# Side work in pairs behind two units' scores, and another order at the ending, in a fused differential attention and feed-forward kernel

## The chip, the cores and the metric

The kernel runs on one core of a Trainium2 chip. The metric is the time of one execution on the device in microseconds. Engine names: TensorE (PE) multiplies, VectorE (DVE) and GpSimd (POOL) do elementwise work, ScalarE (ACT) evaluates functions such as the exponential, and SP only issues transfers (DMAs). Every engine works through its own list in order and waits on semaphores.

## The reference

One sequence of 1024 rows of 256 numbers is normalised and goes through two branches, whose results are added to the input:

```python
xn = layernorm(x)
qkv = xn @ Wqkv                       # q1, k1, q2, k2: 16 heads of 8; v: 16 heads of 16
A1 = causal_softmax(q1 k1) v
A2 = causal_softmax(q2 k2) v
diff = A1 - lam * A2                  # lam from four small vectors
diff = (1 - LAMBDA_INIT) * diff / rms(diff)
attn = diff @ Wproj
ffn  = (gelu(fp8(xn) @ fp8(Wg0)) * (fp8(xn) @ fp8(Wg1))) @ fp8(Wlinear)
out  = x + attn + ffn
```

## The kernel before

**Start.** The rows are normalised and transposed; queries and keys of the first branch are projected and split into an upper and a lower part (`upper` on ScalarE copies the upper part, `rest` on VectorE subtracts it, L621 to 626). `x_to_fp8` (L628) casts the normalised rows in two halves for the feed-forward. The feed-forward's first product runs as 16 steps (L951 to 972), each four products on TensorE, a Gelu on ScalarE (L473) and a gated product on VectorE (L644). Step n waits for the gated product of the last step in the same PSUM banks: the first three steps have banks of their own, and the fourth waits for the first's gated product.

**Attention.** The scores of 2 branches x 4 groups of heads are cut into 96 *units* (12 for each of 8 groups). A unit is three banks of 512 scores. For each unit TensorE computes scores (`scores`, L1027, three or six products, one for each stretch of keys, in row tiles of 32 x 128), ScalarE takes one exponential of 128 x 1536 (L497), and GpSimd zeroes what lies above the diagonal. Units use two sets of three PSUM banks in turn, so the scores of unit n wait for the exponential of unit n - 2 (`exp_done`, L1040).

**Side work.** After the scores of unit n TensorE does that unit's *side work* in column tiles of 128 x 32: `values_due` (L1106) multiplies exponentials of an earlier unit with the values into bank 6, from where VectorE takes them (`take`, L719), and `beside` (L974) does projections that the tables `V_AT`, `QK_AT`, `NORM_AT` and `DOWN_AT` assign to the unit: values, queries and keys of the second branch, norms, and the feed-forward's second product. The tables are written by hand so that nearly every unit has one chunk of values or something of that size. Each float32 product is two passes on TensorE. The loop is in `attention` (L1114).

**Ending.** After the last exponential, TensorE (`ending`, L1141) finishes the values and projects them: `project(b, p)` for 8 blocks b of rows and two halves p of the heads. The products with p = 0 need nothing new; those with p = 1 wait for VectorE to have turned the last group's result back (`turn_back`, L766, which counts `out_t_ready`). ScalarE copies blocks 0, 1 and 6 out of PSUM (`whole`, L501) and between them takes the square root on which the last 16 blocks of rows wait (L513). VectorE adds the residual to the other blocks (L879, L882), and SP and ScalarE send the result out.

## Time and profile before

| | |
|---|---|
| median of 3 runs | 184.3 us (184.03 to 184.45) |
| the profiled execution | 184.12 us, its span 182.3 us |
| TensorE busy | 175.5 us, 96% |
| ScalarE busy | 163.2 us, 90% |
| VectorE busy | 92.4 us, 51% |
| GpSimd busy | 63.5 us, 35% |
| exponentials (L497) | 97 of them, 138.1 us together |
| granted TensorE clock | 0.999 of 2.4 GHz |

The span is from the first to the last instruction. Busy shares are averages over three stages: the start up to the first exponential at 32.9 us, the attention up to the end of the last exponential at 171.2 us, and the ending. The end of a matmul is modelled in the trace, so TensorE looks denser than it is; starts are to be trusted more.

### The profile page before, as it was taken

What the parts mean: (1) busy time and instruction counts of PE and PEld (TensorE: products, weight loads), DVE (VectorE), ACT (ScalarE), POOL (GpSimd) and SP (SyncE); (2) the same over time, 40 slices, a digit from 0 to 9 for tenths busy, and PEclk for the clock granted to TensorE, in tenths of its full rate; (3) what the DMA queues carried; (4) which work ended last, traced back from release to release, by engine and by line L of the source; (5) the groups of instructions that cost most, each with busy time, mean ns of one, the idle gap of its engine ahead of it and who ended that gap; (6) DMA issues with size and microseconds to landing.
All of it is one profiled execution on the core that took longest, in us unless ns stands there. A gap on an engine that the chain in (4) does not pass through costs nothing.

```text
span 182.3 us, 4305 instructions
## 1 busy us (share of the span) xinstructions
PE 175.5 (96%) x1816; PEld 76.3 (42%) x1816; DVE 92.4 (51%) x219; ACT 163.2 (90%) x146; POOL 63.5 (35%) x81
## 2 busy tenths in 40 slices
PE   6999999999999999999999999999999999989992
PEld 6785344543332333343234434334524434432481
DVE  1878789312233230640374121706542789979982
ACT  3586678999999999999999999999999999999820
POOL 8449920052017322360622063217303560323000
PEclk9999999999999999999999999999999999999999
DMA  5996888780000000000277875000000000000015
GB/s 152 382 333 227 219 197 201 175 189 19 0 0 5 0 0 4 0 4 0 42 204 179 210 173 127 0 0 4 4 0 0 4 0 4 0 0 4 0 58 180
DMA packets 8935, 15.02 MB, mean 82 GB/s; under 512 B 2000, under 2 KB 5584, under 8 KB 8912
## 3 DMA queue, kind: packets, MB, share of 16 engines
q1 hardware_dynamic: 8080, 13.92, 28.0%
q10 hardware_dynamic: 832, 0.79, 1.3%
q8 instruction: 16, 0.26, 0.6%
q14 instruction: 7, 0.06, 0.1%
HBM read 5.26 MB, written 1.05 MB: 35 GB/s over the span
## 4 chain that ended last, share of the span: by engine, by line
PE 82%; DVE 11%; ACT 2%; DMA 2%; issue 1%; DVEq 0%
PE ps L1062 35%; PE ps L1050 20%; PE ps L904 12%; PE ps L970 7%; PE ps L1098 4%; DVE o_t L719 2%; PE ps L914 2%; DMA x_sb<-L_attn_x 2%; DVE parts L625 1%; PE ps L894 1%; PE ps L1103 1%; DVE parts L737 1%; ACT L455 1%; DVE area L630 1%; DVE xn_t L763 1%
## 5 line engine op out<-in xcount | busy, mean ns | idle before, releaser
L497 ACT ACTIVATE probs<-ps,shift 128x1536 f32<-128x1536 f32 (+1 forms) x97 | 138.1, 1582 | 0.2 <-PE ps L1050 0.2
L1062 PE MATMUL ps<-probs,v_all 128*32 128x512 f32 (+3 forms) x776 | 78.1, 492 | 1.0 <-DVE o_t L719 0.8
L393 POOL TENSOR_SCALAR_AFFINE_SELECT probs<-probs 128x1024 f32<-128x1024 f32 (+1 forms) x40 | 36.7, 918 | 94.9 <-ACT probs L497 94.8
L1050 PE MATMUL ps<-q_st,k_st 32*128 32x512 f32 (+3 forms) x384 | 48.3, 411 | 0.0
L1050 PEld LDWEIGHTS ps<-q_st,k_st 32*128 32x128 f32 x384 | 22.5, 182 | 61.5 <-ACT probs L497 43.4
L719 DVE STREAM_TRANSPOSE o_t<-ps 128x512 f32<-128x512 f32 x16 | 11.5, 717 | 45.0 <-PE ps L1062 45.0
L1062 PEld LDWEIGHTS ps<-probs,v_all 128*32 128x32 f32 x776 | 16.4, 108 | 18.7 <-issue 9.7
L970 PE MATMUL ps<-area 128*128 128x512 fp8e4 x64 | 14.4, 379 | 0.2 <-DVE parts L625 0.2
L473 ACT ACTIVATE probs<-ps 128x512 bf16<-128x512 f32 x16 | 9.6, 597 | 3.7 <-PE ps L970 3.1
L644 DVE TENSOR_TENSOR area<-ps,probs 128x512 fp8e4<-128x512 f32 x16 | 10.9, 685 | 1.9 <-ACT probs L473 1.7
L970 PEld LDWEIGHTS ps<-area 128*128 128x128 fp8e4 x64 | 6.0, 98 | 8.0 <-issue 0.8
L355 POOL TENSOR_TENSOR squares<-parts 128x512 bf16<-128x512 f32 x8 | 8.6, 1094 | 2.1 <-DVE parts L784 2.1
L904 PE MATMUL ps<-area 128*32 128x256 fp8e4 x256 | 9.2, 273 | 0.0
L784 DVE CAST parts<-ps 128x512 fp32r<-128x512 f32 x4 | 2.8, 692 | 12.5 <-PE ps L904 12.5
L904 PE MATMUL ps<-xn_t,w_q 128*32 128x256 f32 (+1 forms) x88 | 9.0, 482 | 0.0
L904 PE MATMUL ps<-w_q,xn_t 128*32 128x256 f32 x128 | 8.4, 384 | 0.0
L914 PE MATMUL ps<-xn_t,w_q 128*128 128x256 f32 x32 | 8.0, 390 | 0.1
L1098 PE MATMUL ps<-w_p,squares 128*128 128x256 f32 x32 | 7.6, 386 | 0.2 <-DVE squares L768 0.2
L904 PEld LDWEIGHTS ps<-area 128*32 128x32 fp8e4 x256 | 6.7, 97 | 2.3 <-issue 0.5
L789 DVE CAST ffn<-ps 128x512 bf16<-128x512 f32 x4 | 2.8, 691 | 9.2 <-PE ps L904 9.2
L362 POOL CAST area<-probs 128x512 fp8e4<-128x512 f32 x8 | 4.9, 657 | 4.7 <-DVE probs L595 4.7
L1098 PEld LDWEIGHTS ps<-w_p,squares 128*128 128x128 f32 x32 | 5.9, 190 | 1.5 <-DVE squares L768 0.6
(90 smaller groups left out, 126.5 us busy)
## 6 DMA issues: line engine op xcount, KB each, us to landing
q_st<-parts SPq DMA_DIRECT2D x32, 128.0 KB, 2.8
k_st<-parts SPq DMA_DIRECT2D x32, 128.0 KB, 2.8
probs<-L_ffn_w_gating SPq DMA_DIRECT2D x4, 512.0 KB, 7.6
probs<-L_ffn_w_linear SPq DMA_DIRECT2D x1, 1024.0 KB, 12.4
out<-probs SPq DMA_DIRECT2D x3, 256.0 KB, 2.3
x_sb<-L_attn_x ACTq DMA_DIRECT2D x2, 256.0 KB, 5.1
w_q<-L_attn_Wqkv SPq DMA_DIRECT2D x1, 512.0 KB, 9.4
w_q<-L_attn_Wqkv SPq DMA_DIRECT2D x1, 256.0 KB, 4.2
```

What stands on the lines that cost most here:

```text
L355: pool.tensor_tensor(squares[:, i, cols], parts_f32[:, i, 0, cols], parts_f32[:, i, 0, cols], ALU.mult).then_inc(squared, 1)
L393: pool.affine_select(out=blocks, in_=blocks, pattern=pattern, compare_op=ALU.is_ge, fill=0.0, base=0, channel_multiplier=-1).then_inc(mask ...
L473: act.activation(gated[:, n % RING, :], ps[:, 2 * PAIR[n], :], ACT.Gelu_apprx_tanh).then_inc(gelu_ready, 1)
L497: act.activation(probs[:, at:at + PER_UNIT, cols], ps[:, 3 * (n % 2):3 * (n % 2) + 3, cols], ACT.Exp, bias=shift[:, br, 1, hg * BR + br:hg ...
L644: dve.tensor_tensor(hidden[:, c, h * HALF:(h + 1) * HALF], ps[:, 2 * PAIR[n] + 1, :], gated[:, n % RING, :], ALU.mult, saturate=False).the ...
L719: dve.transpose(o_t[:, h, :, :].rearrange("p b w -> p (b w)"), ps[:, 6, :]).then_inc(o_taken, 1)
L904: ins = pe.matmul(ps[q:q + 32, bank, at:at + right.shape[-1]], left[:, q:q + 32], right, start=start, stop=stop, skip_group_check=True)
L914: return pe.matmul(ps[:, bank, at:at + wide], w_q[:, k, i * P:(i + 1) * P], xn_t[:, k, h * HALF + at:h * HALF + at + wide], start=(k == 0 ...
L970: ins = pe.matmul(ps[:, 2 * PAIR[n] + g, :], w_gate8[:, g, k, c * P:(c + 1) * P], x8[:, k, h * HALF:(h + 1) * HALF], start=(k == 0), stop= ...
L1050: ins = pe.matmul(ps[:, bank, at:at + wide * P], k_st[rows, g % STACKS, kb * P:(kb + 1) * P], q_st[rows, g % STACKS, queries], start=True, ...
L1062: ins = pe.matmul(ps[32 * j:32 * j + 32, 6, q0 % HALF:q0 % HALF + wide * P], v_all[:, g % HG, kb, 32 * j:32 * j + 32], probs[:, slot + j, ...
L1098: return pe.matmul(ps[:, Y_BANK[b], at:at + C], out_t[:, p, b * P:(b + 1) * P], w_p[:, p, :], start=start, stop=(p == 1), skip_group_check ...
```

## The change

It has five parts. `JOINED` is the set of 37 even units; for such a unit nothing follows its scores, and its side work is done behind the scores of the odd unit after it, ahead of that unit's own. The value projection of block 1 moves ahead of the first scores. The second `x_to_fp8` moves behind the last two `rest`. In the ending TensorE first does what needs no new turn, then the products with p = 1 one pair after the other, and VectorE turns the first 16 columns of blocks as 8 and 8, the second 8 behind the last difference. The last transfer goes from SP's list to ScalarE's.

```diff
-V_AT = {0: (1, 2), 1: (3,), 2: (4,), 3: (5,), 4: (6,), 5: (7,)}
+V_AT = {0: (2,), 1: (3,), 2: (4,), 3: (5,), 4: (6,), 5: (7,)}
...
+JOINED = {n for n in range(0, 86, 2) if n % STEPS != 8 or n > 60} - {78}
...
-            sp.wait_ge(y_added, 3)
-            sp.dma_start(out_rows[:, 7, :], y[:, 7, :]).then_inc(y_out, 16)
...
             act.dma_start(out_rows[:, 6, :], y[:, 6, :]).then_inc(y_out, 16)
+            act.wait_ge(y_added, 3)
+            act.dma_start(out_rows[:, 7, :], y[:, 7, :]).then_inc(y_out, 16)
...
             rest(1, QK_BANK[1])
-            x_to_fp8(1)
             rest(2, QK_BANK[2])
             rest(3, QK_BANK[3])
+            x_to_fp8(1)
...
-            turn_back(1, 0, 16)
+            turn_back(1, 0, 8)
             take(7, 1)
             difference(3, 1).then_inc(ms_ready, 1)
+
+            turn_back(1, 8, 8)
             dve.wait_ge(rms_ready, 1)
...
                     project_values(0)
+                    project_values(1)
                 for n in range(n0, n0 + BRANCH):
                     scores(n, general)
-                    values_due(n, HG if general and br == 1 else 0, GROUPS)
-                    beside(n)
+                    if n in JOINED:
+                        continue
+                    for m in (n - 1, n) if n - 1 in JOINED else (n,):
+                        values_due(m, HG if general and br == 1 else 0, GROUPS)
+                        beside(m)
...
+                pe.wait_ge(res_ready, TB // 2)
+                residual(6, start=True)
+                project(6, 0)
+                project(2, 0, start=True)
+                project(3, 0)
+                project(4, 0, start=True)
+                project(5, 0)
+                project(7, 0, start=True)
                 pe.wait_ge(out_t_ready, 3)
                 project(0, 1)
                 project(1, 1).then_inc(y_ready, 1)
-                project(2, 0, start=True)
-                project(3, 0)
+                pe.wait_ge(out_t_ready, 4)
                 project(2, 1)
                 project(3, 1).then_inc(y_ready, 1)
-                project(4, 0, start=True)
-                project(5, 0)
-                project(7, 0, start=True)
-                project(6, 0, start=True)
-                pe.wait_ge(res_ready, TB // 2)
-                residual(6)
-                pe.wait_ge(out_t_ready, 4)
+                pe.wait_ge(out_t_ready, 5)
                 project(4, 1)
                 project(5, 1).then_inc(y_ready, 1)
-                pe.wait_ge(out_t_ready, 5)
+                pe.wait_ge(out_t_ready, 6)
                 for b in (6, 7):
                     project(b, 1).then_inc(y_ready, 1)
```

TensorE's list around units 16 and 17, a pair of the change. L1050 are scores (`q_st`, `k_st`), L1062 values (`probs`, `v_all`), L904 a projection. Before:

```order
L1050 MATMUL ps<-q_st,k_st 128x512 [waits exp_done]
L1050 MATMUL ps<-q_st,k_st 128x512 x2
L1062 MATMUL ps<-probs,v_all 32x512 [waits exp_done]
L1062 MATMUL ps<-probs,v_all 32x512 x3
L1050 MATMUL ps<-q_st,k_st 128x512 [waits exp_done]
L1050 MATMUL ps<-q_st,k_st 128x512 x2
L904 MATMUL ps<-xn_t,w_q 32x512 [waits low_ready]
L904 MATMUL ps<-xn_t,w_q 32x512 x3
```

The same two units now, four lines further down in the file:

```order
L1054 MATMUL ps<-q_st,k_st 128x512 [waits exp_done]
L1054 MATMUL ps<-q_st,k_st 128x512 x2
L1054 MATMUL ps<-q_st,k_st 128x512 [waits exp_done]
L1054 MATMUL ps<-q_st,k_st 128x512 x2
L1066 MATMUL ps<-probs,v_all 32x512 [waits exp_done]
L1066 MATMUL ps<-probs,v_all 32x512 x3
L908 MATMUL ps<-xn_t,w_q 32x512 [waits low_ready]
L908 MATMUL ps<-xn_t,w_q 32x512 x3
```

Both units' scores stand first, each with its own wait for an exponential, and the two pieces of side work follow as one.

VectorE's list at the start, from the first gated halves on: L630 is `x_to_fp8`, L625 `rest`, L644 a gated product. Before:

```order
L630 CAST area<-xn_t 128x2x512 [waits xt_out]
L625 TENSOR_TENSOR parts<-ps,parts 128x512 [waits hi_ready]
L618 COPY xn_t<-ps 128x2x256 [waits xt_ready]
L625 TENSOR_TENSOR parts<-ps,parts 128x512 [waits hi_ready]
L630 CAST area<-xn_t 128x2x512 [waits xt_out]
L625 TENSOR_TENSOR parts<-ps,parts 128x512 [waits hi_ready] x2
L644 TENSOR_TENSOR area<-ps,probs 128x512 [waits gelu_ready] x3
```

The same stretch now:

```order
L632 CAST area<-xn_t 128x2x512 [waits xt_out]
L627 TENSOR_TENSOR parts<-ps,parts 128x512 [waits hi_ready]
L620 COPY xn_t<-ps 128x2x256 [waits xt_ready]
L627 TENSOR_TENSOR parts<-ps,parts 128x512 [waits hi_ready] x3
L632 CAST area<-xn_t 128x2x512 [waits xt_out]
L646 TENSOR_TENSOR area<-ps,probs 128x512 [waits gelu_ready] x3
```

The second cast stands directly ahead of the first gated product.

TensorE's list at the ending, behind the last values: L1098 is `project`, L1103 `residual`. Before:

```order
L1098 MATMUL ps<-w_p,squares 128x256 [waits out_t_ready]
L1098 MATMUL ps<-w_p,squares 128x256 x9
L1103 MATMUL ps<-x_sb,ident 128x256 [waits res_ready]
L1098 MATMUL ps<-w_p,squares 128x256 [waits out_t_ready]
L1098 MATMUL ps<-w_p,squares 128x256
L1098 MATMUL ps<-w_p,squares 128x256 [waits out_t_ready]
L1098 MATMUL ps<-w_p,squares 128x256
```

And now:

```order
L1107 MATMUL ps<-x_sb,ident 128x256 [waits res_ready]
L1102 MATMUL ps<-w_p,squares 128x256 x6
L1102 MATMUL ps<-w_p,squares 128x256 [waits out_t_ready]
L1102 MATMUL ps<-w_p,squares 128x256
L1102 MATMUL ps<-w_p,squares 128x256 [waits out_t_ready]
L1102 MATMUL ps<-w_p,squares 128x256
L1102 MATMUL ps<-w_p,squares 128x256 [waits out_t_ready]
L1102 MATMUL ps<-w_p,squares 128x256
L1102 MATMUL ps<-w_p,squares 128x256 [waits out_t_ready]
```

The first two products with p = 1, which fill blocks 0 and 1, were first and are now eighth and ninth. ScalarE's list at the ending now:

```order
L508 ACT_TABLE_LOAD
L508 ACTIVATE newton<-newton 128x1
L505 ACTIVATE probs<-ps 128x256 [waits y_ready] x2
L513 ACTIVATE newton<-newton,root_eps 128x16 [waits ms_ready,eps_set]
L505 ACTIVATE probs<-ps 128x256 [waits y_ready]
L517 DMA out<-probs 128x256 [waits y_copied]
L519 DMA out<-probs 128x256 [waits y_added]
```

Before, it had the same rows without the last. The two copies at L505 are those of blocks 0 and 1, and L513 is the square root.

## Rows read from the trace of the kernel before

**Rows 1.** The page: busy time (us, share of span, instructions); chain by engine.
```profile
PE 175.5 (96%) x1816; PEld 76.3 (42%) x1816; DVE 92.4 (51%) x219; ACT 163.2 (90%) x146; POOL 63.5 (35%) x81
...
PE 82%; DVE 11%; ACT 2%; DMA 2%; issue 1%; DVEq 0%
```
**Rows 2.** The page's groups: busy us, mean ns | idle us before, released by.
```profile
L497 ACT ACTIVATE probs<-ps,shift 128x1536 f32<-128x1536 f32 (+1 forms) x97 | 138.1, 1582 | 0.2 <-PE ps L1050 0.2
```
**Rows 3.** Timeline of ScalarE (start us, us, engine, line), units 1, 46, 68, 94.
```profile
34.63 1.54 ACT L497 ACTIVATE probs<-ps,shift 128x1536 f32<-128x1536 f32 x1 [0.22 <-PE ps L1050]
...
99.29 1.58 ACT L497 ACTIVATE probs<-ps,shift 128x1536 f32<-128x1536 f32 x1
...
130.59 1.77 ACT L497 ACTIVATE probs<-ps,shift 128x1536 f32<-128x1536 f32 x1
...
168.08 1.56 ACT L497 ACTIVATE probs<-ps,shift 128x1536 f32<-128x1536 f32 x1
```
**Rows 4.** Timeline, exponential of unit 40 and scores of unit 42.
```profile
90.75 1.54 ACT L497 ACTIVATE probs<-ps,shift 128x1536 f32<-128x1536 f32 x1
...
92.38 0.50 PE L1050 MATMUL ps<-q_st,k_st 32*128 32x512 f32 x4
```
**Rows 5.** Timeline, scores and exponential of unit 22.
```profile
64.38 0.50 PE L1050 MATMUL ps<-q_st,k_st 32*128 32x512 f32 x3
...
64.93 1.54 ACT L497 ACTIVATE probs<-ps,shift 128x1536 f32<-128x1536 f32 x1
```
**Rows 6.** Timeline of TensorE, units 0 to 2.
```profile
31.77 0.50 PE L1050 MATMUL ps<-q_st,k_st 32*128 32x512 f32 x3
32.20 1.93 PE L904 MATMUL ps<-w_q,xn_t 128*32 128x256 f32 x32
34.06 0.50 PE L1050 MATMUL ps<-q_st,k_st 32*128 32x512 f32 x5
34.50 1.07 PE L904 MATMUL ps<-w_q,xn_t 128*32 128x256 f32 x16
35.50 0.51 PE L1050 MATMUL ps<-q_st,k_st 32*128 32x384 f32 x6
```
**Rows 7.** Timeline of the start: casts, GpSimd's product, gated product, third and fourth step.
```profile
11.34 0.68 DVE L630 CAST area<-xn_t 128x1024 fp8e4<-128x1024 f32 x1
...
15.13 1.03 POOL L355 TENSOR_TENSOR squares<-parts 128x512 bf16<-128x512 f32 x1
...
15.39 1.32 DVE L630 CAST area<-xn_t 128x1024 fp8e4<-128x1024 f32 x1
...
17.84 0.67 DVE L644 TENSOR_TENSOR area<-ps,probs 128x512 fp8e4<-128x512 f32 x1
...
18.06 1.89 PE L970 MATMUL ps<-area 128*128 128x512 fp8e4 x8 [0.15 <-DVE parts L625]
```
**Rows 8.** Timeline of the ending.
```profile
171.51 0.40 PE L1062 MATMUL ps<-probs,v_all 128*32 128x256 f32 x4
...
172.07 4.58 PE L1098 MATMUL ps<-w_p,squares 128*128 128x256 f32 x20 [0.16 <-DVE squares L768]
...
173.24 0.66 ACT L505 ACTIVATE probs<-ps 128x256 f32<-128x256 f32 x2 [0.50 <-PE ps L1098]
174.97 0.31 ACT L513 ACTIVATE newton<-newton,root_eps 128x16 f32<-128x16 f32 x1 [1.07 <-DVE newton L741]
...
176.57 0.45 DVE L768 STREAM_TRANSPOSE squares<-xn_t 128x256 f32<-128x256 f32 x1
...
178.85 0.42 DVE L882 TENSOR_TENSOR probs<-ps,x_sb 128x256 f32<-128x256 f32 x1 [0.17 <-PE ps L1098]
...
179.55 0.50 SPq L328 DMA_DIRECT2D out<-probs  x1
```
**Rows 9.** DMA issues: queue, count, KB each, median us to landing.
```profile
out<-probs ACTq DMA_DIRECT2D x1, 128.0 KB, 2.7
out<-probs SPq DMA_DIRECT2D x1, 128.0 KB, 2.4
```

## The prediction, made before the changed kernel ran

> **What bounds the kernel now.** I read three views in this order: busy time and the chain, then the groups by line, then the timeline around single units. The first misleads. TensorE is busy 96% of the span and the chain that ended last gives it 82% [rows 1], so the reader would take TensorE for the bound and anything that shortens its stream for a gain. But ScalarE's 97 exponentials (L497) cover 138.1 us and ScalarE sat idle before them for 0.2 us in all [rows 2]. Two streams are full at once. Which one sets the pace has to come from places where they part.
>
> ScalarE alone: unit 41 has little side work (four short norm products), so TensorE comes early to the scores of unit 42 and is ahead until unit 68. There the exponential that starts at 99.29 (unit 46) ends at 100.87, and the one that starts at 130.59 (unit 68) at 132.36 [rows 3]: 31.49 us over 22 units, 1.431 us each. The starts come a little faster (31.30 us, 1.423 each) and the records grow from 1.58 to 1.77, so starts run ahead and ends show the true rate. Now the whole stretch: the end of unit 1 is 34.63 + 1.54 = 36.17, that of unit 94 is 168.08 + 1.56 = 169.64 [rows 3]: 133.47 us over 93 units, 1.435 each. At 1.431 it would have been 133.1. **The exponentials run within 0.4 us of ScalarE's own rate: a shorter TensorE stream can give 0.4 us there and no more.**
>
> Three delays tie the engines together, and the change leans on all of them.
> - Scores of unit n need the exponential of n-2 finished (its PSUM banks). When TensorE waits for nothing else: the exponential of unit 40 ends at 90.75 + 1.54 = 92.29, scores of 42 start at 92.38 [rows 4]: 0.09 us.
> - From the start of a unit's scores to the end of its exponential, when ScalarE was waiting: scores of 22 start at 64.38, the exponential ends at 64.93 + 1.54 = 66.47 [rows 5]: 2.09 us. Unit 1 gives 2.11 (34.06 to 36.17), and there the row itself says that ScalarE waited for TensorE [rows 3, 6].
> - Scores take 0.43 us of TensorE (31.77 to 32.20) [rows 6]. Side work of two units in one piece is there already, behind the scores of unit 0: two value projections, 32.20 until the next scores at 34.06, 1.86 us. Side work of one unit: 34.50 to 35.50, 1.00 us [rows 6]. The second half of the large piece thus costs 0.86, and 0.14 us of every piece is going in and out of it.
>
> **The change, part by part: the 37 pairs.** The even unit's side work goes behind the odd unit's scores. Gained on TensorE: one passage in and out per pair, 0.14 us, 37 x 0.14 = 5.2 us of TensorE time. Lost: the odd unit's scores cannot start until the exponential of the unit before the pair has ended, and now 1.86 us of side work is queued behind that wait, with the next pair's scores behind it. Say the exponential of n-1 ends at 0 (n even, pair n and n+1). Scores of n+1 start at 0.09, side work at 0.52, scores of n+2 at 2.38, and the exponential of n+2 ends at 2.38 + 2.09 = 4.47. ScalarE without a gap would have ended n, n+1 and n+2 at 1.43, 2.86 and 4.29. So it waits 0.18 us. The lateness is handed on with a lag: exponential n+3 ends 1.43 after, at 5.90, and n+3 stands two pairs behind n-1, so a pair takes 2.95 us against 2.87 (2 x 1.435) now: 0.08 per pair, 37 x 0.08 = 3.0 us. The pairs come in runs of 4, 5, 5, 5, 5, 10 and 3 between unpaired units, and a run of odd length ends on a full 0.18 instead of half of it; five such runs add some 0.3. **Term: +3.3 us.** Bounds: below, the 0.14 us is kept and nothing is late, so ScalarE's 0.4 us are gained (-0.4); above, every pair pays its 0.18 in full, 6.7 us. I take the middle, since the handing-on follows from the order and the rows behind the three delays are direct.
>
> The Trainium skill (TensorEngine Tiling (Array Packing), Key Properties) says that changing the tiling mode, and not merely the tile, drains TensorE. The trace agrees by the 0.14 us, since scores use 32 rows and side work 32 columns [rows 6]. By that rule alone the pairs would be worth those 5.2 us; rival 2 is what would have to hold for it.
>
> **Value projections ahead of the first scores.** Block 1's 0.86 us now runs before the scores of unit 0, which had 32.20 - 31.77 = 0.43 us and a table load to hide in. The first exponential moves by about 0.3 us later, but unit 1's scores then stand ready at once, where ScalarE waited 0.22 [rows 3] and more before: unit 1 ends where it did. Cost 0.
>
> **Head: fp8 cast of x's second half behind the last two subtractions.** Now the cast takes 15.39 to 16.71, the subtractions end at 17.91 and the feed-forward's third step starts 0.15 later at 18.06 [rows 7]. Without the cast ahead, the subtractions are held by ScalarE's copies and end about 0.4 us earlier; the third step then starts at 17.75, straight after the second. But the cast now stands ahead of the first gated product, which ran 17.84 to 18.51 [rows 7] and which the fourth step waits for (same banks). The cast took 0.68 us when GpSimd was idle at its start and 1.32 when a GpSimd product was running [rows 7]: it began its work only when that product ended (15.13 + 1.03 = 16.16), and needed 0.55 from there. At its new place, 17.5, the fourth such product runs until about 18.16 (the third starts as the second ends, at 16.13, and each takes 1.03). So the cast ends at 18.71, the gated product at 19.33, the fourth step starts at 19.48 and not 18.92 (half of the 1.89 row's eight steps behind 18.06). From there to the first exponential the feed-forward is one dense TensorE stream (0.86 us a step), so the shift arrives whole. **Term: +0.55 us**; from +0.1 (the cast at 0.68) to +0.7.
>
> The Trainium skill (SBUF — State Buffer, SBUF: two separate sides) says that VectorE and GpSimd share a port pair that one of them locks for a whole instruction, the other blocking fully. The trace agrees: 1.32 against 0.68. Without such a lock the term would be +0.1.
>
> **Ending, TensorE.** Now TensorE's last product with values starts at 171.51 and the first projection at 172.07, held by VectorE's turn; then 30 half-products run dense (the row of 20: 4.58 = 0.32 for the first, 18 of 0.216, 0.38 for the last) to 178.81 [rows 8]. With untied ones first it starts one round of 0.216 and some 0.11 for leaving the column tiles behind 171.51, at 171.84: 0.23 earlier. **But block 0 and 1's results come last of 18 instead of first of 4:** 171.84 + 0.32 + 16 x 0.216 + 0.38 = 176.0. ScalarE's queue holds the two copies of these results (173.24 to 173.90) *ahead* of the square root at 174.97 [rows 8]. The copies now start at 176.03, the root follows 0.56 behind at 176.6 instead of 174.97: +1.62. Behind it on VectorE hang the reciprocal, two scalings and two turns; the last turn ended 177.02 [rows 8], 2.05 behind the root's start; now 178.64. TensorE stands at the second last of these turns (0.65 earlier, 177.99), then has 8 half-products: 178.05 + 0.32 + 6 x 0.216 + 0.38 = 180.04 against 178.81: +1.23. The addition of block 7 ends at 180.5, not 179.27.
>
> **Turning in halves.** The first half saves less than 0.3 us ahead of the last take of values, but that take waits for the last product anyway, which ends at 171.51 + 0.40 = 171.91. The second half, 0.45 us, lies in the wait for the root. Cost 0.
>
> **Last transfer.** It was issued at 179.55 on SP, 0.28 behind the addition [rows 8]. ScalarE's queue has nothing else to issue by then and goes an estimated 0.05 behind (what other waits take): 180.54, +0.99. The queue's own transfer of that size took 2.7 us to land against SP's 2.4 [rows 9], so between 0 and 0.3 more. **Term for the ending: +1.15 us** (0.99 to 1.3).
>
> **Sum.** 3.3 + 0.55 + 1.15 = 5.0. The profiled execution took 184.12 us (182.3 of span), the median of the three runs is 184.3; 189.1 and 189.3.
>
> **Rivals.**
> 1. *The pairs are hidden.* The wait of the odd scores falls into slack and ScalarE stays dense: -0.4 in the body, head and ending as above: 184.3 + 1.3 = 185.6. For it: TensorE is 5 us shorter. Against: 0.09 + 0.43 + 1.86 + 2.09 = 4.47 is more than three exponentials.
> 2. *TensorE is the bound after all, as the chain of waits has it.* ScalarE's 1.43 us would be TensorE's pace shown through, each pair gives back its 0.14: -5.2 + 1.7 = -3.5, 180.8 us: faster. It decides from 0.05 us kept per pair (1.7 / 37). Against: in units 42 to 45 TensorE waited for ScalarE, and the ends came no faster than 1.43.
> 3. *The root is not held,* because the copies' results come earlier than I count: the ending then gains 0.5 (0.23 and 0.25) in place of losing 1.15: 187.7. Against: the order on both queues is plain.
> 4. *Each pair pays in full:* 184.3 + 6.7 + 1.7 = 192.7, if the next pair cannot make use of the lateness.
>
> **Chances.** Forecast 0.68 (188.2 to 190.3), rival 1 0.08, rival 2 0.06, rival 3 0.09, rival 4 0.05, and 0.04 for no change by terms that cancel. Range 186.9 to 190.6. Changes under 0.2% (0.4 us) are what a measurement cannot tell from none here. Faster 0.06, same 0.03, slower 0.91.
>
> **What would show it.** In the profile after: TensorE idle before the odd units' scores, some 0.2 to 0.5 us each; starts of exponentials alternating between 1.43 and up to 1.6; the exponentials' group (L497 now) with idle time of 2 to 4 us released by TensorE's scores instead of 0.2; the fourth feed-forward step at 19.5; the square root at the end starting right behind two copies, not behind VectorE's reduction; some 12.2 us from the last exponential's end to the span's end against 11.1. I am wrong if the exponentials' ends keep coming every 1.43 us, or if the square root still starts within 0.2 us of VectorE's last sum of squares.

## The result, and the profile after

The changed kernel takes 190.72 us (median of 4 runs, 189.68 to 190.85), the kernel before 184.32 (184.03 to 184.45): a ratio of 1.0337, interval 1.0298 to 1.0376. It is slower, as forecast (189.3), by 1.4 us more than forecast. The profiled execution took 190.61 us, its span is 188.9, so the sum of the terms, 5.0, stands against 6.5 between the two profiled executions. The granted clock is full in both traces.

To see where the 6.5 us arose I cut both spans at three events: the start of the feed-forward's first product, the end of unit 1's exponential, and the end of unit 94's.

| stretch | before | after | difference | predicted |
|---|---|---|---|---|
| up to the feed-forward's first product | 16.02 | 16.26 | +0.24 | none |
| from there to the end of exponential 1 | 20.16 | 20.73 | +0.57 | +0.55 |
| to the end of exponential 94 | 133.46 | 137.47 | +4.01 | +3.3 |
| to the span's end | 12.68 | 14.42 | +1.74 | +1.15 |
| span | 182.32 | 188.88 | +6.56 | +5.0 |

The first line is the load of the input: it lay between 15.97 and 17.4 in the traces of this study, in kernels that are the same up to there, so it is not counted for the change.

The page of the changed kernel, first busy time, then the chain, then two groups of section 5, against [rows 1, 2]:

```profile
PE 173.3 (92%) x1816; PEld 79.9 (42%) x1816; DVE 92.1 (49%) x220; ACT 165.4 (88%) x146; POOL 63.9 (34%) x81
...
ACT 52%; PE 35%; DVE 6%; DMA 3%; issue 1%; SPq 0%; DVEq 0%; ACTq 0%
...
L497 ACT ACTIVATE probs<-ps,shift 128x1536 f32<-128x1536 f32 (+1 forms) x97 | 140.3, 1531 | 2.0 <-PE ps L1054 1.6
...
L1054 PE MATMUL ps<-q_st,k_st 32*128 32x512 f32 (+3 forms) x384 | 47.7, 410 | 6.1 <-ACT probs L497 4.7
```

TensorE is busy 2.2 us less and its scores now wait 6.1 us, 4.7 of them for exponentials. ScalarE waits 2.0 us before its exponentials, ten times as long as before. The chain, which gave TensorE 82%, now gives ScalarE 52%. TensorE's shorter stream did not shorten the kernel; it shows as waiting.

A pair and its neighbours, in the timeline of TensorE (columns as in [rows 3]; scores of units 24, 25, then 26 and 27 in one row):

```profile
66.83 1.92 PE L1066 MATMUL ps<-probs,v_all 128*32 128x512 f32 x16
68.69 0.50 PE L1054 MATMUL ps<-q_st,k_st 32*128 32x512 f32 x3
69.38 0.50 PE L1054 MATMUL ps<-q_st,k_st 32*128 32x512 f32 x5 [0.19 <-ACT probs L497]
69.81 1.07 PE L1066 MATMUL ps<-probs,v_all 128*32 128x128 f32 x16
70.70 1.04 PE L908 MATMUL ps<-xn_t,w_q 128*32 128x512 f32 x8
71.67 1.10 PE L1054 MATMUL ps<-q_st,k_st 32*128 32x384 f32 x12
```

and of ScalarE around them:

```profile
67.79 2.98 ACT L497 ACTIVATE probs<-ps,shift 128x1536 f32<-128x1536 f32 x2
...
69.23 2.97 ACT L497 ACTIVATE probs<-ps,shift 128x1536 f32<-128x1536 f32 x2
...
72.22 1.54 ACT L497 ACTIVATE probs<-ps,shift 128x1536 f32<-128x1536 f32 x1
```

Of two exponentials in one row the first ends 1.54 after its start: that of 67.79 at 69.33. The odd unit's scores start at 69.38, 0.05 behind it (row with 0.19 of waiting); then the side work of two units, 69.81 to 71.67, which is 1.86 us as in [rows 6]; then the next even unit's scores, whose exponential starts at 72.22 and ends at 73.76, 2.09 behind them as in [rows 5]. The exponential ahead of that is the second in the row of 69.23 and started at 70.67 (its end, 72.20, less 1.53), so this step is 1.55 where the others around it are 1.44. One start in four is late, not every second one. That is what the prediction's chain gives, since it runs from the exponential of n-1 to that of n+3, over four units and two pairs. With the measured 0.05 it is 0.05 + 0.43 + 1.86 + 2.09 + 1.43 = 5.86 us; the trace has 75.19 - 69.33 = 5.86 from the end of exponential 23 to that of 27. Four units took 5.72 to 5.74 before, so a pair loses 0.07 us.

One place was not in it. TensorE at units 43 to 47:

```profile
95.74 0.51 PE L1054 MATMUL ps<-q_st,k_st 32*128 32x384 f32 x6 [0.81 <-ACT probs L497]
...
101.12 0.64 PE L1066 MATMUL ps<-probs,v_all 128*32 128x256 f32 x8 [1.14 <-DVE o_t L721]
...
102.13 0.73 PE L1054 MATMUL ps<-q_st,k_st 32*128 32x512 f32 x6
```

and VectorE, GpSimd and ScalarE there:

```profile
95.85 0.69 DVE L531 TENSOR_REDUCE norm_most<-ps 128x1 f32<-128x512 f32 x1
...
97.28 0.55 DVE L549 TENSOR_TENSOR norm_most<-norm_most 32x1 f32<-32x1 f32 x1
...
98.96 0.78 DVE L569 TENSOR_SCALAR shift<-shift 32x8 f32<-32x8 f32 x1
99.77 0.55 DVE L574 COPY shift<-shift 32x8 f32<-32x8 f32 x3
100.35 0.72 DVE L721 STREAM_TRANSPOSE o_t<-ps 128x512 f32<-128x512 f32 x1
```
```profile
97.19 0.64 POOL L393 TENSOR_SCALAR_AFFINE_SELECT probs<-probs 128x512 f32<-128x512 f32 x1 [3.29 <-ACT probs L497]
98.62 1.10 POOL L393 TENSOR_SCALAR_AFFINE_SELECT probs<-probs 128x1024 f32<-128x1024 f32 x1 [0.80 <-ACT probs L497]
```
```profile
102.68 1.54 ACT L497 ACTIVATE probs<-ps,shift 128x1536 f32<-128x1536 f32 x1 [1.11 <-PE ps L1054]
```

VectorE empties bank 6 (the take, L721) and then works out the second branch's bounds from norms, a chain of small instructions (L531 to L574), before its next take. The values of unit 40 now come a unit later, so the chain begins later, and it is longer: 4.48 us (95.85 to 100.33) where it was 3.45. All of the 1.03 lies in two tiny instructions that run beside GpSimd's masks. L549 starts at 97.28 and ends with the mask at 97.83, L569 starts at 98.96 and ends with the next at 99.7; before they took 0.15 and 0.16. Then the first ended before the mask at 95.22 began, and the second ran between that mask and the next (at 96.65). The next take starts at 100.35, and TensorE's values of unit 45, which want the same bank, wait 1.14 us. ScalarE loses 1.11 us in one go. Before, TensorE waited 0.33 us at the same place, and its lead there hid it:

```profile
93.25 0.69 DVE L529 TENSOR_REDUCE norm_most<-ps 128x1 f32<-128x512 f32 x1
...
96.73 0.72 DVE L719 STREAM_TRANSPOSE o_t<-ps 128x512 f32<-128x512 f32 x1
```
```profile
97.50 0.64 PE L1062 MATMUL ps<-probs,v_all 128*32 128x256 f32 x8 [0.33 <-DVE o_t L719]
```

The start after, VectorE and TensorE, against [rows 7]:

```profile
17.70 1.26 DVE L632 CAST area<-xn_t 128x1024 fp8e4<-128x1024 f32 x1
18.89 1.87 DVE L646 TENSOR_TENSOR area<-ps,probs 128x512 fp8e4<-128x512 f32 x3
```
```profile
19.71 1.02 PE L974 MATMUL ps<-area 128*128 128x512 fp8e4 x4 [0.69 <-DVE area L646]
```

The cast takes its long form (1.26, predicted 1.21) and the fourth step waits 0.69 us for the gated product behind it.

The ending after, ScalarE, against [rows 8]:

```profile
180.85 0.66 ACT L505 ACTIVATE probs<-ps 128x256 f32<-128x256 f32 x2 [3.30 <-PE ps L1102]
181.40 0.31 ACT L513 ACTIVATE newton<-newton,root_eps 128x16 f32<-128x16 f32 x1
184.45 0.38 ACT L505 ACTIVATE probs<-ps 128x256 f32<-128x256 f32 x1 [2.75 <-PE ps L1102]
184.87 0.37 ACTq L517 DMA_DIRECT2D out<-probs  x1
185.34 0.75 ACTq L519 DMA_DIRECT2D out<-probs  x1
```

VectorE's last addition and SP's issues:

```profile
184.88 0.42 DVE L886 TENSOR_TENSOR probs<-ps,x_sb 128x256 f32<-128x256 f32 x1 [0.17 <-PE ps L1102]
```
```profile
184.05 2.06 SPq L328 DMA_DIRECT2D out<-probs  x2
```

The root starts right behind the two copies, 6.94 us after exponential 94's end. The last addition ends 10.85 us after it, against 9.63 before. Both stand where the prediction put them (176.6 and 180.5 less 169.64 are 6.96 and 10.86). The last transfer is issued 10.88 us after it, against 9.91: 0.97 later, where the prediction had 0.99. But that transfer then takes 3.1 us to land (issue to landing in the profile) and not 2.4 as before. The 0.97 and these 0.77 are the 1.74 of the tail.

### The profile page after: what moved, and what is told of

The parts are those of the page before. It is cut to its first block, busy times and chain, and to the rows that moved or that the text cites. A ratio compares the mean times of both kernels' runs of the same rounds, so it can differ in the third digit from the quotient of the medians.

```text
span 188.9 us, 4306 instructions
## 1 busy us (share of the span) xinstructions
PE 173.3 (92%) x1816; PEld 79.9 (42%) x1816; DVE 92.1 (49%) x220; ACT 165.4 (88%) x146; POOL 63.9 (34%) x81
## 4 chain that ended last, share of the span: by engine, by line
ACT 52%; PE 35%; DVE 6%; DMA 3%; issue 1%; SPq 0%; DVEq 0%; ACTq 0%
ACT probs L497 51%; PE ps L1066 10%; PE ps L974 6%; PE ps L1054 6%; PE ps L908 4%; PE ps L1102 3%; PE ps L918 3%; DMA x_sb<-L_attn_x 3%; DVE o_t L721 1%; PE ps L1107 1%; PE ps L898 1%; DVE area L632 1%; DVE shift L569 0%; DVE norm_most L531 0%; DVE parts L627 0%
## 5 line engine op out<-in xcount | busy, mean ns | idle before, releaser
L497 ACT ACTIVATE probs<-ps,shift 128x1536 f32<-128x1536 f32 (+1 forms) x97 | 140.3, 1531 | 2.0 <-PE ps L1054 1.6
L1066 PE MATMUL ps<-probs,v_all 128*32 128x512 f32 (+3 forms) x776 | 73.6, 489 | 1.7 <-DVE o_t L721 1.6
L1054 PE MATMUL ps<-q_st,k_st 32*128 32x512 f32 (+3 forms) x384 | 47.7, 410 | 6.1 <-ACT probs L497 4.7
L721 DVE STREAM_TRANSPOSE o_t<-ps 128x512 f32<-128x512 f32 x16 | 11.5, 717 | 49.0 <-PE ps L1066 48.9
L1066 PEld LDWEIGHTS ps<-probs,v_all 128*32 128x32 f32 x776 | 18.8, 109 | 27.3 <-issue 19.0
L786 DVE CAST parts<-ps 128x512 fp32r<-128x512 f32 x4 | 2.8, 692 | 12.8 <-PE ps L908 12.8
L908 PE MATMUL ps<-w_q,xn_t 128*32 128x256 f32 x128 | 7.7, 382 | 0.0
L362 POOL CAST area<-probs 128x512 fp8e4<-128x512 f32 x8 | 5.4, 720 | 4.8 <-DVE probs L597 4.8
```

Source lines behind the costliest of these rows:

```text
L497: act.activation(probs[:, at:at + PER_UNIT, cols], ps[:, 3 * (n % 2):3 * (n % 2) + 3, cols], ACT.Exp, bias=shift[:, br, 1, hg * BR + br:hg ...
L721: dve.transpose(o_t[:, h, :, :].rearrange("p b w -> p (b w)"), ps[:, 6, :]).then_inc(o_taken, 1)
L908: ins = pe.matmul(ps[q:q + 32, bank, at:at + right.shape[-1]], left[:, q:q + 32], right, start=start, stop=stop, skip_group_check=True)
L1054: ins = pe.matmul(ps[:, bank, at:at + wide * P], k_st[rows, g % STACKS, kb * P:(kb + 1) * P], q_st[rows, g % STACKS, queries], start=True, ...
L1066: ins = pe.matmul(ps[32 * j:32 * j + 32, 6, q0 % HALF:q0 % HALF + wide * P], v_all[:, g % HG, kb, 32 * j:32 * j + 32], probs[:, slot + j, ...
```

## The experiments

Stretches are those of the table above; of the first one nothing is counted. "Tail" is the last of them. Times are medians, each against runs of the kernel before on the same chip.

**1. The pairs alone.**

```diff
+JOINED = {n for n in range(0, 86, 2) if n % STEPS != 8 or n > 60} - {78}
...
-                    values_due(n, HG if general and br == 1 else 0, GROUPS)
-                    beside(n)
+                    if n in JOINED:
+                        continue
+                    for m in (n - 1, n) if n - 1 in JOINED else (n,):
+                        values_due(m, HG if general and br == 1 else 0, GROUPS)
+                        beside(m)
```

> The kernel before with the 37 pairs alone (side work of the even unit behind the odd unit's scores; nothing else changed). My theory, the odd scores' wait with two units of side work queued behind it: the traces of before and after put the attention at 133.5 and 137.5 us from the end of unit 1 to the end of unit 94, so this run should take 4.0 us more than before, 188.3 (187.5 to 189.0), and its exponentials should again stall at units 46 and 84. Rival, that the pairs cost little and the loss sits in the other parts: 184 to 185.5. Rival, that TensorE is the bound and each pair gives back its 0.14 us: below 184.

Measured: 188.64 us, ratio 1.0213 (1.018 to 1.0245), as expected, with the stall at unit 46. The attention takes 137.51 us, as in the changed kernel (137.47); the tail is as before (12.77). The ratio is worth 3.9 us, more than the 3.3 of the forecast, and the pairs alone make the kernel slower: rivals 1 and 2 fall. Not all of the 4.05 us in the attention is loss. Unit 0 is a pair, so unit 1's scores stand ready earlier, and from the feed-forward's first product to the end of exponential 1 it takes 19.80 us (before 20.16). From that product to the end of exponential 94 the pairs cost 3.69 us.

**2. Everything but the pairs.**

```diff
-JOINED = {n for n in range(0, 86, 2) if n % STEPS != 8 or n > 60} - {78}
+JOINED = set()
```

> The changed kernel with the set of pairs empty. My theory: head +0.57 us (cast ahead of the first gated product), ending +1.76 as in the trace of after (12.68 to 14.44 us from the end of unit 94 to the end of the span), body as before: 184.3 + 2.3 = 186.6 (186.0 to 187.2). One thing is open: without pairs the second projection ahead of the first scores has nothing behind it in unit 0, so 0 to 0.3 less. Rival, that parts interact and the pairs only lose because of the new start: 184.3 to 185.

Measured: 186.75 us, 1.0114 (1.0088 to 1.014), as expected. Attention 133.48 (before 133.46), start +0.55, tail 14.66. Pairs and the rest add up: by the medians 4.1 and 2.2 us beside 6.4 together. By stretches they don't. The start is -0.36 and +0.55, yet +0.57 together, and the tail +0.09 and +1.98, yet +1.74 together; the two differences cancel.

**3. The ending's order alone** (TensorE's new ending and the turn in halves, on the kernel before; last transfer on SP).

```diff
+                residual(6, start=True)
+                project(6, 0)
...
                 pe.wait_ge(out_t_ready, 3)
                 project(0, 1)
                 project(1, 1).then_inc(y_ready, 1)
...
-            turn_back(1, 0, 16)
+            turn_back(1, 0, 8)
```

> The kernel before with TensorE's and VectorE's new ending alone (untied products first, turning in halves); the last transfer stays on SP. My theory, the square root stands behind two copies in ScalarE's queue and those wait for products that are now eighth and ninth: last addition +1.2 us, and SP's last issue right behind it instead of 0.28 later, so 184.3 + 1.0 = 185.3 (184.9 to 185.7). Rival, that the ending's order costs nothing and the 1.76 us of after come from the last transfer: 184.0 to 184.3.

Measured: 186.07 us, 1.0068 (1.0041 to 1.0095), above the 184.9 to 185.7 expected; tail 14.71, 2.0 us longer than before. The last addition is 1.22 us later, as expected. The rest comes behind it. The order alone carries the ending's whole loss.

**4. The same with the square root ahead of the two copies.**

```diff
-            for b in (0, 1):
-                whole(b)
             act.wait_ge(eps_set, 2)
             act.wait_ge(ms_ready, 1)
             act.activation(newton[:, 3, 112:128], ... ACT.Sqrt ...).then_inc(rms_ready, 1)
+            for b in (0, 1):
+                whole(b)
```

> The same ending with one edit more: ScalarE takes the square root ahead of the two copies of blocks 0 and 1. My theory: the root is back right behind VectorE's last sum of squares, the turns come as before, TensorE ends its 30 half products 0.2 to 0.3 us earlier: 184.3 - 0.2 = 184.1 (183.8 to 184.4). If the loss of the ending's order is something else than the root (the turning in halves, the waits on TensorE), this run stays at 185.0 to 185.7.

Measured: 185.03 us, 1.0023 (1.0008 to 1.0038); tail 13.34. This lies above the 183.8 to 184.4 expected, at the foot of the range for "something else than the root". The time alone doesn't decide, but the trace does. The root starts 5.33 us after exponential 94's end, as before, and the tail is 1.37 us shorter than kernel 3's (1.04 by the medians): the copies' hold on the root is shown. The last addition now ends 0.23 us *earlier* than in the kernel before, as the forecast's first step had it, and still the kernel is 0.4 us slower. What is left lies behind the last addition (3.93 us). Its issues on SP and the stretch by microsecond (window, its length, busy us of PE, PEld, DVE, ACT and POOL with their instructions, granted clock, share of the 16 DMA engines in use, GB/s):

```profile
178.14 1.17 SPq L326 DMA_DIRECT2D out<-probs  x2
179.53 1.38 SPq L328 DMA_DIRECT2D out<-probs  x1
```
```profile
178.00:179.00 1.00, 1.00 (x5) 0.57 (x3) 0.80 (x2) 0.35 (x1) 0.00 (x0) 1.00 0.79 259
179.00:180.00 1.00, 0.04 (x1) 0.00 (x0) 0.42 (x1) 0.03 (x1) 0.00 (x0) 1.00 0.94 305
180.00:181.00 1.00, 0.00 (x0) 0.00 (x0) 0.00 (x0) 0.00 (x0) 0.00 (x0) 1.00 1.00 333
181.00:182.00 1.00, 0.00 (x0) 0.00 (x0) 0.00 (x0) 0.00 (x0) 0.00 (x0) 1.00 0.45 153
```

The DMA engines are in use for 0.79, 0.94 and 1.00 of three microseconds, and the last issue stands 1.38 us on SP. In this kernel the transfer of blocks 0 and 1 is close by as well: it is issued 7.08 us after exponential 94's end, 0.97 ahead of the next, where it went at 4.28 before. So all five transfers, 1 MB, are issued within 2.4 us.

**5. Half the bytes.** Kernel 4 with the same transfers, each of the first 128 of 256 columns; the other half of the output isn't sent.

```diff
-                sp.dma_start(out_rows[:, b:b + 2, :], y[:, b:b + 2, :]).then_inc(y_out, 16)
+                sp.dma_start(out_rows[:, b:b + 2, 0:C // 2], y[:, b:b + 2, 0:C // 2]).then_inc(y_out, 16)
```

> The ending with the root first, and every output transfer sends the left half of each row only (half the output is not written); as many issues and rows as before. With the root first the last addition ended 9.41 us behind unit 94 (9.63 before), yet the end came 13.34 behind it (12.68 before), with the DMA engines at 1.00 of their time and 333 GB/s for one microsecond. Theory, the output's bytes crowd at the end: with half of them no issue waits, and the span ends 12.3 to 12.6 behind unit 94. Rival, issues wait for one another whatever their size: it stays at 13.1 to 13.5.

Measured: 183.73 us, 0.9971 (0.9957 to 0.9984); tail 12.13, below what was expected. The first of the three rows is SP's last issue, the others two of the microseconds:

```profile
179.22 0.72 SPq L328 DMA_DIRECT2D out<-probs  x1
```
```profile
179.00:180.00 1.00, 0.00 (x0) 0.00 (x0) 0.19 (x1) 0.00 (x0) 0.00 (x0) 1.00 0.67 186
180.00:181.00 1.00, 0.00 (x0) 0.00 (x0) 0.00 (x0) 0.00 (x0) 0.00 (x0) 1.00 0.48 138
```

The same instructions end at the same places and the tail shrinks by 1.21 us. The number and order of the transfers is not the cause, their bytes are. The last transfer lands 2.3 us after its issue and not 3.5. How close the transfers meet differs. The last four, 768 KB, are issued within 1.93 us before, but within 1.29 in the changed kernel, since the root's hold delays the first issue of the four by 1.61 us and the last by only 0.97. That this is the whole of the changed kernel's 0.77 is argued from the rows; the bytes were halved in kernel 4's ending only. Nor is the end bound to the first of the four: from its issue to the span's end the traces have 4.70 (before), 4.83 (changed), 5.11 (kernel 3), 5.30 (kernel 4) and 6.38 us (kernel 12, below), no fixed time.

**6. The last transfer alone on ScalarE's queue.**

```diff
-            sp.wait_ge(y_added, 3)
-            sp.dma_start(out_rows[:, 7, :], y[:, 7, :]).then_inc(y_out, 16)
...
+            act.wait_ge(y_added, 3)
+            act.dma_start(out_rows[:, 7, :], y[:, 7, :]).then_inc(y_out, 16)
```

> The kernel before with block 7's transfer issued by ScalarE instead of SP, nothing else. Two theories. Prediction's: it goes 0.25 us sooner and lands up to 0.3 later, -0.25 to +0.05. New one, from the endings so far, in which 4.3 to 4.9 us pass from the issue of blocks 2 and 3 to the last landing whichever queue issues: the last 768 KB move at some 180 GB/s and the queue of the last issue changes nothing, 0 +- 0.15. Rival, that ScalarE's queue is slower for the second transfer in a row (its issue took 0.75 and 1.24 us in two traces): +0.4 to +0.8.

Measured: 184.68 us, 1.0005 (0.999 to 1.0019): no change. The rival is out; the two theories lie too close together to be told apart. The issue starts 0.25 us earlier (9.66 after exponential 94's end, before 9.91), and the tail is 12.88 (before 12.68). The Trainium skill (Trainium Kernel Development and Optimization, Key Constraints) says that transfers of all queues share the same engines and that a second issuing engine saves only issue time; the trace agrees as far as it goes: the issue is earlier, and even that saving is not seen in the time.

**7. The cast alone.**

```diff
             rest(1, QK_BANK[1])
-            x_to_fp8(1)
             rest(2, QK_BANK[2])
             rest(3, QK_BANK[3])
+            x_to_fp8(1)
```

> The kernel before with the second cast alone moved behind the last two subtractions. My theory, the first gated product stands behind the cast and the fourth feed-forward step behind the product: from the first feed-forward step to the end of unit 1's exponential 20.7 us instead of 20.16, time +0.55 (184.7 to 185.3 against 184.4 or so). Rival, that the earlier third step makes up for it: no change or 0.3 less.

Measured: 184.78 us, 1.0011 (0.9995 to 1.0026). The trace has the full shift: from the feed-forward's first product to the end of exponential 1 it takes 20.67 us (before 20.16), with the cast at 1.25:

```profile
17.41 1.25 DVE L630 CAST area<-xn_t 128x1024 fp8e4<-128x1024 f32 x1
```
```profile
19.41 0.81 PE L970 MATMUL ps<-area 128*128 128x512 fp8e4 x3 [0.68 <-DVE area L644]
```

The time shows 0.2 us of it; the interval reaches 0.5. That the stretch grew is shown three times (here, in kernel 2 and in the changed kernel: 0.51, 0.55 and 0.57); whether the whole of it reaches the end of the kernel is open, since the load at the start (15.97 to 17.4 in the traces) and the tail (12.54 here, 12.68 before) vary too.

**8. The pairs without units 40 and 82.** These two are the ones whose values stand ahead of the norms and of the residual's product.

```diff
-JOINED = {n for n in range(0, 86, 2) if n % STEPS != 8 or n > 60} - {78}
+JOINED = {n for n in range(0, 86, 2) if n % STEPS != 8 or n > 60} - {78, 40, 82}
```

> The pairs alone, without the pairs (40, 41) and (82, 83). In the traces with pairs TensorE stands 1.14 us before unit 45's second half for a take that VectorE does only behind its chain on the norms of unit 41, and unit 84 loses 0.3 to a residual product behind two units of side work. My theory: without these two the 35 others cost their 0.07 each, so 1.3 to 1.6 us less than the pairs alone, +2.6 over before (2.3 to 3.0). If the stall at unit 45 comes from something else (the pair 44/45 is not one, the chain is long in any case) it stays at +3.8 to +4.1.

Measured: 187.09 us, 1.0136 (1.0107 to 1.0166), as expected and 1.55 less than kernel 1; the attention 136.38, 1.13 less. At the place of the 1.14 us wait its TensorE has none, and L549 and L569 take 0.15 and 0.16 again, since they now run clear of the masks:

```profile
99.27 0.64 PE L1064 MATMUL ps<-probs,v_all 128*32 128x256 f32 x8
```

So these two pairs, the one at the norms above all, made over a quarter of the loss in the attention. The 35 that are left make the attention 136.38 - 133.46 = 2.92 us longer, but 0.33 of this is the start that exponential 1 gained (19.83 us for 20.16), so they cost 2.59 us, 0.074 each. In the run of ten pairs, from the end of exponential 57 to that of 77, it is 29.36 us for 28.62: 0.073 each. The prediction had 0.08.

**9 and 10. Half the value products, with and without pairs.** Both kernels take only the first half of each product's columns, so part of the sums is left out. TensorE's side work becomes shorter and its order stays. Kernel 9, without pairs, is the control of kernel 10, with them.

```diff
-                    ins = pe.matmul(ps[32 * j:32 * j + 32, 6, q0 % HALF:q0 % HALF + wide * P],
+                    ins = pe.matmul(ps[32 * j:32 * j + 32, 6, q0 % HALF:q0 % HALF + wide * P // 2],
```

Without pairs:

> The kernel before with the same halved products, no pairs: the control of the run above. By my theory ScalarE bounds the attention and TensorE has slack already, so halving its value products gives only the 0.3 to 0.4 us by which the exponentials missed ScalarE's own 1.431 us a unit: 133.1 us from the end of unit 1 to that of unit 94 instead of 133.5, and 183.7 to 184.4 in all (the ending's values are halved too, about 0.5 less). Rival, that TensorE paces the exponentials: units of 1.0 us less side work by 0.43 for three of four units, 25 to 30 us less.

With pairs:

> The pairs alone, and every product with values takes the left half of its columns only (part of the sums is left out). Side work of a pair of two value chunks falls from 1.86 to about 1.0 us. My theory: the odd scores' wait costs only because 1.86 us stand behind it; 0.05 + 0.43 + 1.0 + 2.09 = 3.6 is under three exponentials (4.29), so such pairs are free. From the end of unit 1 to the end of unit 94 at most 1.5 us over the same kernel without pairs (unit 45's chain remains, and pairs with a projection are in between). Rival, that each pair costs its 0.08 by the waiting itself, whatever stands behind: 3 to 4 us over.

Measured without pairs: 184.79 us, 1.0021 (1.0004 to 1.0038), a little above the 183.7 to 184.4 expected. Three executions took 184.5 to 185.05 us with a mean granted clock of 0.97 to 0.99. The profiled one took 189.4 with 0.92, since its clock fell on the way. A long window ahead of that and one in it (columns as above):

```profile
45.00:89.00 44.00, 35.99 (x457) 13.88 (x453) 14.06 (x23) 44.00 (x32) 14.29 (x16) 1.00 0.00 1
93.00:109.00 16.00, 16.00 (x176) 7.42 (x177) 5.14 (x20) 13.12 (x9) 2.38 (x3) 0.50 0.74 193
```

In the first the clock is full and TensorE is busy 36.0 of 44 us, where it was 43.9 in the kernel before, with ScalarE busy throughout. From the end of exponential 1 to that of 41 it takes 57.28 us, before 57.54. Taking 18% of TensorE's time away gains 0.26 us there. If TensorE had set the pace, 18% of the attention would be an estimated 24 us. **ScalarE sets it**, and rival 2 is dead apart from any pair. In the second window the clock is at 0.50, TensorE is busy throughout and ScalarE is the one that waits: 18.03 us from the end of exponential 43 to that of 53, before 14.31.

Measured with pairs: 189.46 us, 1.0266 (1.0231 to 1.0301), where at most 1.5 us over the kernel without pairs was expected for the attention; it takes 137.82 us, 4.36 more than in the kernel before. The expectation was missed. The trace says why: first the row of ScalarE for units 10 to 17, then the windows around unit 18:

```profile
48.97 11.58 ACT L499 ACTIVATE probs<-ps,shift 128x1536 f32<-128x1536 f32 x8
```
```profile
57.00:59.00 2.00, 1.26 (x11) 0.59 (x15) 0.00 (x0) 2.00 (x3) 1.67 (x3) 0.72 0.04 12
59.00:61.00 2.00, 2.00 (x16) 0.20 (x5) 1.40 (x3) 1.55 (x2) 0.86 (x1) 0.50 0.00 0
61.00:63.00 2.00, 1.91 (x38) 1.09 (x34) 0.00 (x0) 1.27 (x1) 0.00 (x0) 0.93 0.00 0
```
```profile
59.23 1.94 PE L906 MATMUL ps<-xn_t,w_q 128*32 128x512 f32 x8
```

Eight exponentials in 11.58 us are 1.42 to 1.43 from start to start, through four pairs: with short side work a pair costs nothing, which is what the prediction's arithmetic says (0.09 + 0.43 + 2.09 leaves room for 1.68). But TensorE now idles (it was busy 1.26 of 2 us in the first window), the granted clock goes to 0.50, the 1.2 GHz level, and the projection that takes 1.04 us in the changed kernel takes 1.94. The exponential of unit 18 starts 1.4 us late. The same happens at units 24, 62, 64, 66 and 95. Exponential by exponential against the kernel before, units 18, 24, 62, 64 and 66 lose 3.76 us, each of them in or right behind a stretch with the clock at 0.50. Unit 46 loses 0.60; VectorE's chain is late here too, with one copy (L574) that takes 0.95 us for 0.16, to the end of a mask. Units 2 and 6 lose 0.38, behind an exponential 1 that ends 0.33 earlier, and the others together gain 0.37. So where the clock is full these pairs cost nothing, and the kernel's time cannot be used as their measure.

**11 and 12. Two attempts to keep the good part.** In the kernel before, TensorE waits 0.16 us at 172.07 [rows 8]. Kernel 11 puts the residual's product into that gap and leaves the rest as it was; kernel 12 also adds blocks 2 and 3 on VectorE ahead of the reciprocal.

```diff
                 values_due(UNITS + 1, 0, GROUPS)
+                pe.wait_ge(res_ready, TB // 2)
+                residual(6, start=True)
                 pe.wait_ge(out_t_ready, 3)
...
-                project(6, 0, start=True)
-                pe.wait_ge(res_ready, TB // 2)
-                residual(6)
+                project(6, 0)
```

> The kernel before with block 6's residual product moved into TensorE's 0.45 us gap behind the last values, and nothing else: blocks 0 and 1 stay ahead of everything else and ScalarE's copies come 0.2 later. Expected: the last addition 0.2 earlier; 0.2 us less in all if the transfers keep their spacing, 0 if they crowd.

> A try to beat the kernel before: no pairs, its cast and its queues; VectorE adds the residual to blocks 2 and 3 in the wait for the square root and not behind the last turns, and TensorE does block 6's residual product in its 0.45 us gap behind the last values. If the ending is set by moving the last output (768 KB from the issue of blocks 2 and 3 on, at 177.6 now): that issue comes 2 us sooner, the rest by 0.2, 0.3 to 0.5 us less than before. If it is set by TensorE's dense run alone: 0.2 less. If neither: no change.

Measured: kernel 11 184.66 us, 1.0021 (1.0007 to 1.0035); kernel 12 184.62 us, 0.9995 (0.9983 to 1.0007). Neither beats the kernel before, and kernel 11 is slightly slower. Its last addition does end 0.2 us earlier, but the issue behind blocks 2 and 3 stands 1.2 us for 0.8, and the tail is 12.80. In kernel 12 VectorE waits for the sums of block 3 and the turns come later by it (before, the reciprocal ran at 175.3, 5.7 us after exponential 94's end; here 6.2):

```profile
175.97 0.69 DVE L793 TENSOR_TENSOR probs<-ps,x_sb 128x512 f32<-128x512 f32 x1 [0.36 <-PE ps L1101]
176.58 0.24 DVE L879 RECIPROCAL newton<-newton 128x16 f32<-128x16 f32 x1
```
```profile
176.69 3.25 SPq L326 DMA_DIRECT2D out<-probs  x2
```

Blocks 2 and 3 are issued at 176.69, 6.32 us after exponential 94's end and 1.66 earlier than before, and the last transfer is issued 0.1 earlier too, yet the tail is 12.70 us (before 12.68). Sending the first of the last four sooner is worth nothing here.

## Why the forecast was right, and where it was short

**Which engine bounds.** Right, and shown by kernel 9 and by kernel 1, in which TensorE's stream is shorter and the kernel slower. The reading against the chain (82% TensorE) held. Why the chain followed TensorE before is not shown; both streams were full, and ScalarE's idle time of 0.2 us left little to tell them apart.

**The pair's arithmetic.** Right in its mechanism: 1.86 of side work, 2.09 to the end of the exponential, and one late step in two pairs. From exponential to scores it is 0.05 and not 0.09, which makes the pair 0.07 us and not 0.08, as measured. The 37 pairs' own part is thus 2.6 to 2.7 us for 3.0, and that the whole term came out above 3.3 is the stall of the next paragraph. The 0.14 us per piece is gained on TensorE, and spent waiting. The Trainium skill (TensorEngine Tiling (Array Packing), Key Properties) has the drain that this saves, without a price; that a passage costs 0.14 us here agrees with it, and saving it was worth nothing, since the engine that it frees is not the bound. The 0.3 us for runs of odd length was not needed (by the prediction's own 0.18 and 0.08 it would have been 0.4).

**Failed: that the pairs touch only the two engines.** The step "the exponential of n+2 ends at 4.47" takes the side work as dense. Behind one pair, (40, 41), it isn't: TensorE waits 1.14 us for VectorE's take behind the norm chain, +1.1 us, which kernel 8 shows by taking that pair out (and unit 82's, whose residual product cost unit 84 some 0.3). By the rows 1.03 of it is VectorE standing behind GpSimd's masks, since the chain was pushed onto them; no kernel here moved the masks alone, so this share is read and not tested. The prediction listed three delays that tie TensorE and ScalarE together, and left out the fourth, bank 6 with VectorE behind it. The row with 0.33 us of waiting was in the trace of before at that place; it was the sign that this chain was nearly late already.

**The value projections and the cast.** The cast's term is right: 0.51 (kernel 7) for 0.55. The projections' "Cost 0" holds without pairs, where kernel 2's stretch at the start is kernel 7's within 0.04 us. With pairs it does not fit: the pair at unit 0 had already brought the end of exponential 1 forward by 0.36 us (kernel 1), and the projection ahead of the first scores takes that back. By the traces, -0.36 for the pair and 0.51 for the cast leave 0.42 of the changed kernel's 0.57 to it. The prediction set the projection's price against ScalarE's wait before exponential 1, a wait that the pair removes anyway; it counted neither this gain nor this price, and its total for the start is right because they cancel. No kernel here adds the projection alone to the pairs, so the 0.42 is a difference and not tested. The long form of the cast came again at 1.25 and 1.26, in each case beside a GpSimd product. The prediction had used this contention for the cast and had not asked for it anywhere else.

**The ending, on the engines.** Right to 0.02 us: copies, root, last addition and last issue. Rival 3 is out; kernel 4 shows that the root was held, and what by.

**Failed in size: the ending's transfers.** The term "between 0 and 0.3 more" took the last transfer by itself, and took its landing time from a trace in which the transfers lie further apart. It measured 0.77 more, behind transfers that meet in the end; kernel 5 shows for kernel 4's ending that their bytes are what costs. The whole ending measured 1.74 (changed kernel) to 2.0 us (kernels 2 and 3) for 1.15.

**The sum.** With 4.0 for the pairs, 0.57 and 1.74 it is 6.3; 184.3 and that are 190.6, beside a median of 190.72, which lies 0.1 us above the range given; by the ratio, 184.3 x 1.0337 = 190.5, it is just inside. The range held up to 1.3 us for two terms that were each missed upward, the pairs by 0.7 and the ending by 0.6. Rival 4, the only case that reached higher, has the attention at +6.7 and did not occur.

**The signs named beforehand.** Starts between 1.43 and up to 1.6 apart: seen (1.44 and 1.55), but with one late start in four. Idle time before the exponentials of 2 to 4 us: 2.0, at the lower end. Idle time before odd scores of 0.2 to 0.5: 6.1 us over 37 pairs, 0.16 each, in most pairs 0.1 or 0.2 in turn, so this was too large. Fourth step at 19.5: 19.71, of which 0.24 is the later load. From the last exponential's end (176.05 in the trace) to the span's end 12.2: it was 12.8, by the transfers.

## What to carry to other kernels

When two engines are both full, take the pace from a stretch where one of them is ahead, and then price every wait in the moved work, including those for an engine that is busy half the time: a wait of a third of a microsecond that is in the trace already is a place where a shift of one step can cost one whole microsecond. Ahead of a move of work in front of a copy, read what stands *behind* that copy on its engine. At the end of a kernel a transfer's landing time depends on what was issued just ahead of it: look at how closely the last ones follow each other, and not only at the last instruction.

## What the runs showed of the hardware

- Issues of output on SP and ScalarE take longer when output crowds: 0.39 to 0.42 us for the first two on SP in every kernel, but 0.81 in the kernel before, 1.37 in the changed kernel and 1.65 in kernel 3 for the one behind blocks 2 and 3, 0.75 for the last one of the changed kernel and 1.38 in kernel 4; with half the bytes 0.72 in place of 1.38.
- The granted clock fell to 0.50, the 1.2 GHz level, in the middle of the attention in both kernels with half the value products, though TensorE was busy some 80% of the time ahead of it. With pairs, its longest wait in the attention ahead of that stretch was 0.93 us. In the traces of the other kernels the clock stayed full there. Taking work off an engine that is not the bound can thus make it the bound.
- Exponentials of 128 x 1536 start every 1.42 to 1.43 us on ScalarE when nothing is late, in every kernel here, while their records grow when the stream is dense.
- Some of VectorE's instructions took longer beside a running GpSimd one: casts of 1.25 and 1.26 for 0.68, and in the norm chain, up to the end of a mask, 0.55, 0.78 and 0.95 for 0.15 to 0.16. The kernel before has such rows too (L735, 1.40 for 0.49 at 159.6). The reductions and transposes beside a mask kept their times (0.17 and 0.72).
